# Linear attention on one core: the first chunk begins with the values, and the identity has a load of its own

## What is computed

```python
xn = _layernorm(x)                      # x: 2048 x 512
q = silu(xn @ Wq); k = silu(xn @ Wk); v = silu(xn @ Wv)
# chunks of 128 tokens, 16 heads of 32
scores = einsum('bchd,bshd->bhcs', qb, kb) * D
o_intra = einsum('bhcs,bshd->bchd', scores, vb)
o_inter = einsum('bchd,bhde->bche', qb, S) * q_decay
S_new = chunk_decay * S + einsum('bshd,bshe->bhde', kb * k_decay, vb)
gate = (xn @ Wg1) @ Wg2
out = rmsnorm_per_head((o_intra + o_inter) * sigmoid(gate)) * w @ Wo
```

## Time and profile before

| | us |
|---|---|
| median of 3 runs | 1657.27 |
| the 3 runs | 1653.48 to 1657.48 |
| profiled execution, its own time | 1654.82 |
| profiled execution, its span | 1653.0 |
| busy: PE / DVE / ACT / POOL | 1547.6 / 997.4 / 593.1 / 640.0 |

### The profile page before, as it was taken

How to read it: one execution, slowest core, us unless ns; L and a number is a source line. 1 busy time by engine, 2 the same in 40 slices (tenths; PEclk the granted TensorE clock), 3 DMA queues, 4 the chain that set the end, 5 groups by cost and what they waited for, 6 DMA issues and landing times. The chain is left out here.

```text
span 1653.0 us, 22088 instructions
## 1 busy us (share of the span) xinstructions
PE 1547.6 (94%) x7906; PEld 1077.0 (65%) x7906; DVE 997.4 (60%) x1719; ACT 593.1 (36%) x1124; POOL 640.0 (39%) x534
## 2 busy tenths in 40 slices
PE   5999899999999999997989999959999998999998
PEld 4887445455544555553767888847777776788887
DVE  7774888787778788863445566545564455232322
ACT  3121245555555555554222222253424232222221
POOL 4000277858868886700336766513120201000000
PEclk9999799999999999999899999979999998999999
DMA  6887645444525464301751222153030231420210
GB/s 234 249 256 205 136 124 120 105 116 133 119 62 161 120 141 102 104 16 45 258 193 58 78 70 64 52 180 128 1 128 1 77 81 61 147 100 3 102 52 26
DMA packets 104299, 182.07 MB, mean 110 GB/s; under 512 B 28696, under 2 KB 45080, under 8 KB 103540
## 3 DMA queue, kind: packets, MB, share of 16 engines
q1 hardware_dynamic: 87032, 119.20, 25.2%
q0 software_dynamic: 13520, 53.85, 11.3%
q10 hardware_dynamic: 3640, 7.61, 1.3%
HBM read 118.62 MB, written 61.74 MB: 109 GB/s over the span
## 5 line engine op out<-in xcount | busy, mean ns | idle before, releaser
L1072 ACT ACTIVATE att_probs<-att_ring 128x512 f32<-128x512 f32 (+3 forms) x640 | 298.1, 536 | 286.8 <-DVE att_ring L1103 142.9
L1094 DVE TENSOR_REDUCE att_maxes<-att_ring 128x2 f32<-128x1024 f32 (+7 forms) x366 | 339.3, 948 | 71.2 <-PE att_ring L992 61.3
L1025 PE MATMUL att_outp<-att_probs,att_vs 128*64 128x512 f32 (+3 forms) x1280 | 276.0, 553 | 0.3 <-ACT att_att L1056 0.3
L1025 PEld LDWEIGHTS att_outp<-att_probs,att_vs 128*64 128x64 f32 x1280 | 79.0, 138 | 122.4 <-issue 70.7
L1804 DVE TENSOR_TENSOR glu_hid<-glu_sig,glu_u 128x512 f32<-128x512 f32 x44 | 30.3, 688 | 140.6 <-PE glu_u L1744 140.6
L1013 PE MATMUL att_ring<-route_wah,route_wbh 102*128 102x512 f32 (+2 forms) x320 | 104.6, 402 | 4.7 <-DVE att_maxes L1094 3.7
L992 PE MATMUL att_ring<-route_wbh,route_wah 100*128 100x512 f32 (+2 forms) x320 | 101.0, 399 | 8.2 <-DVE att_maxes L1094 5.6
L1013 PE MATMUL att_ring<-moew_wal,moew_wbl 102*128 102x512 f32 (+2 forms) x320 | 102.2, 401 | 6.0 <-DVE att_maxes L1094 6.0
L2374 POOL TENSOR_TENSOR lin_sig<-lin_o_copy,lin_sig 128x512 f32<-128x512 f32 x16 | 20.4, 1277 | 208.4 <-ACT lin_o_copy L2234 208.4
L992 PE MATMUL att_ring<-moew_wbl,moew_wal 100*128 100x512 f32 (+2 forms) x320 | 96.2, 377 | 3.8 <-DVE att_maxes L1094 1.9
L1013 PEld LDWEIGHTS att_ring<-route_wah,route_wbh 102*128 102x128 f32 x320 | 55.0, 191 | 67.1 <-issue 39.1
(11 more groups left out here) (294 smaller groups left out, 3457.6 us busy)
## 6 DMA issues: line engine op xcount, KB each, us to landing
att_q_raw<-in_w POOLq DMA_DIRECT2D x48, 352.0 KB, 4.3
w_ternary<-att_q_out POOLq DMA_DIRECT2D x24, 352.0 KB, 2.8
tail_up<-w_ternary SPq DMA_DIRECT2D x22, 256.0 KB, 5.0
xn<-qkv_x SPq DMA_DIRECT2D x4, 1024.0 KB, 7.9
q_hi<-qkv_hi SPq DMA_DIRECT2D x16, 256.0 KB, 3.8
q_lo<-qkv_lo SPq DMA_DIRECT2D x16, 256.0 KB, 4.5
k_hi<-qkv_hi SPq DMA_DIRECT2D x16, 256.0 KB, 2.9
k_lo<-qkv_lo SPq DMA_DIRECT2D x16, 256.0 KB, 3.8
```

The source lines that it names most:

```text
L1025: last = pe.matmul(outp[v_cols(h), off:CH], vs[p % 2][:, kt, v_cols(h)], probs[:, g % 4, h, off:CH], start=kt == 0, stop=kt == TT * (c + 1 ...
L1072: act.activation(probs[:, g % 4, h, off:CH], ring[:, rg.banks["score", g][h], off:CH], ACT.Exp).then_inc(exped, 1)
L1094: last = dve.tensor_reduce(maxes[:, hs, t, g:g + 1], banks[:, :, 0:width], AX.X, ALU.max)
```

## The change

The first chunk of the linear attention is made in the order v, q, k instead of q, k, v (the later chunks keep q, k, v). The weight that is split during the experts' stage is now Wv instead of Wq, and the stage itself splits Wq, Wk, Wg1, Wo in that order. The first chunk's normalised tiles are turned into the PSUM tile `lin_wide` (one bank for each tile) by `first_turn`, not through the ring, and the loop over the tiles of v waits for one tile's low part at a time. The identity stands last in the constants and has a transfer and a semaphore of its own, `ident_in`; TensorE's block begins with the wait for it alone, and the wait for `g2_in` moves to `gates`. On ScalarE a root of `lin_eps` into `lin_warm` stands ahead of the wait for the statistics, and the decays (`q_decay`, `k_decay16`, `c_decay`) now come ahead of the first high parts.

```diff
-    HT, WQ_AT = FT // 2, range(2, 2 + 3 * KT, 3)
+    HT, WV_AT = FT // 2, range(2, 2 + 3 * KT, 3)
...
-            for kind, count, late in (("q", KT, 0), ("k", KT, 0), ("v", TT, 0), ("gk", 1, 0),
-                                      ("norm", TT, -1), ("out", TT, 1), ("turn", KT, 0)):
+            inner = [("q", KT, 0), ("k", KT, 0), ("v", TT, 0)]
+            if c == 0:
+                inner = [inner[2], *inner[:2]]
+            for kind, count, late in (*inner, ("gk", 1, 0), ("norm", TT, -1), ("out", TT, 1), ("turn", KT, 0)):
+                if kind == "norm" and c == -1:
+                    continue
...
-        order = ("k", "v", "g1", "o")
+        order = ("q", "k", "g1", "o")
...
-            for dst, src in ((cst, cst_d[:, P:]), (ld_p, decay_p_d), (nw, norm_w_d)):
-                sp.dma_start(dst[:], src).then_inc(s_in, 16)
+            rest = NC - P
+            sp.dma_start(ident, cst_d[:, P + rest:]).then_inc(ident_in, 16)
+            for dst, src in ((cst[:, 0:rest], cst_d[:, P:P + rest]), (ld_p[:], decay_p_d), (nw[:], norm_w_d)):
+                sp.dma_start(dst, src).then_inc(s_in, 16)
...
-                wait_taken(sp, "norm", c, TT - 1)
+                if c:
+                    wait_taken(sp, "norm", c, TT - 1)
+                else:
+                    sp.wait_ge(first_low, TT)
...
+            def first_turn():
+                for t in range(TT):
+                    pe.wait_ge(norm.normed, t + 1)
+                    for k in range(KT):
+                        last = pe.transpose(wide[:, t, k * P:(k + 1) * P], x[:, t, k * P:(k + 1) * P], ident)
+                    last.then_inc(first_turned, 1)
...
-            pe.wait_ge(s_in, 3 * 16)
-            pe.wait_ge(g2_in, 16)
-            pe.wait_ge(zeroed, 2)
-            norm_turn(0)
+            pe.wait_ge(ident_in, 16)
+            first_turn()
             for c in range(NCH):
-                wait_taken(pe, "norm", c, TT - 1)
+                if c:
+                    wait_taken(pe, "norm", c, TT - 1)
+                else:
+                    for t in range(TT):
+                        pe.wait_ge(first_low, t + 1)
+                        projected("v", 0, t, "v", True)
+                    pe.wait_ge(s_in, 3 * 16)
+                    pe.wait_ge(zeroed, 2)
+                    ws.wait(pe, KT)
...
+            def first_high():
+                for t in range(TT):
+                    act.wait_ge(first_turned, t + 1)
+                    act.activation(xh[:, :, t * P:(t + 1) * P], wide[:, t, :].rearrange("p (k n) -> p k n", n=P), ACT.Copy
+                                   ).then_inc(norm.xh_ready, 1)
...
             act.wait_ge(zeroed, 2)
+            act.activation(warm[:], eps[:], ACT.Sqrt)
             norm.take_root(act, 0)
-            norm_high(0)
-            split(("k",))
             act.wait_ge(s_in, 3 * 16)
...
+            first_high()
+            split(("q",))
+            for t in range(TT):
+                take(v[:, t, :], ACT.Silu, "v", 0, t)
+            split(("k",))
...
                 else:
-                    split(("v", "g1"))
+                    split(("g1",))
...
+            def first_low_parts():
+                for t in range(TT):
+                    s = slice(t * P, (t + 1) * P)
+                    dve.wait_ge(norm.xh_ready, t + 1)
+                    dve.tensor_tensor(xl[:, :, s], wide[:, t, :].rearrange("p (k n) -> p k n", n=P),
+                                      xh[:, :, s].bitcast(F32), ALU.subtract).then_inc(first_low, 1)
...
-    parts += [p == c, P - 1 - p]
+    parts += [P - 1 - p, p == c]
```

More of the change, by code:

```diff
@@ L1388, in experts_stage @@
                                      for n, k in (("gathered", 2), ("fetched", 3), ("stored", 3)))
-        wq_raw = st.sb("wq_raw", [P, D])
-        wq_in, wq_high, wq_low, next_in = (st.sem(n) for n in ("wq_in", "wq_high", "wq_low", "next_in"))
+        wv_raw = st.sb("wv_raw", [P, D])
+        wv_in, wv_high, wv_low, next_in = (st.sem(n) for n in ("wv_in", "wv_high", "wv_low", "next_in"))
         x_turned, xh_ready, xl_ready = st.sem("x_turned"), st.sem("xh_ready"), st.sem("xl_ready")
@@ L1514, in _ @@
                     x_high(j + 2)
[L1515 to L1518, removed]
+                if j in WV_AT:
+                    k = WV_AT.index(j)
+                    act.wait_ge(wv_in, (k + 1) * 16)
+                    act.activation(carried.h[:, k, :], wv_raw[:], ACT.Copy).then_inc(wv_high, 1)
         @block.vector
@@ L1590, in _ @@
                     down_bias(j + 1)
[L1591 to L1595, removed]
+                if j - 1 in WV_AT:
+                    k = WV_AT.index(j - 1)
+                    dve.wait_ge(wv_high, k + 1)
+                    dve.tensor_tensor(carried.l[:, k, :], wv_raw[:], carried.h[:, k, :].bitcast(F32),
+                                      ALU.subtract).then_inc(wv_low, 1)
             finish(NT - 1)
@@ L1871, in lightning_stage @@
         cst = st.sb("cst", [P, NC])
[L1872 removed]
+        at = np.cumsum([0, P, P, P, HD, KT * P, 1, P])
         dist, ld_f = carried.dist[:], carried.ld_f
[L1874 removed]
+        causal, cpos, diag, msel, spread, kpos, ident = (cst[:, a:b] for a, b in zip(at[:-1], at[1:]))
         names = ("q", "k", "v", "o")
         wh, wl = {}, {}
[L1877 to L1878 removed]
+        wh["v"], wl["v"] = carried.h, carried.l
+        for i, n in enumerate(("q", "k")):
             wh[n], wl[n] = kept.weights(i)
@@ L1914, in lightning_stage @@
         s_in, zeroed, expd, masked = st.sem("s_in"), st.sem("zeroed"), st.sem("expd"), st.sem("masked")
-        g2_in = st.sem("g2_in")
+        g2_in, ident_in = st.sem("g2_in"), st.sem("ident_in")
+        first_turned, first_low = st.sem("first_turned"), st.sem("first_low")
         scored, score_taken = st.sem("scored"), st.sem("score_taken")
@@ L2039, in gates @@
                 wait_taken(pe, "gk", c)
+                if c == 0:
+                    pe.wait_ge(g2_in, 16)
                 if c:
@@ L2109, in _ @@
                 if c == 0:
-                    ws.wait(pe, KT)
+                    ws.wait(pe, 2 * KT)
                 for m in range(KT):
@@ L2114, in _ @@
                     spread_inverses(c - 1)
[L2115 to L2118, removed]
+                    for t in range(TT):
+                        projected("v", c, t, "v", True)
                 if c == 0:
@@ L2215, in _ @@
                     act.wait_ge(o_made, c * NI)
+                    for t in range(TT):
+                        take(v[:, t, :], ACT.Silu, "v", c, t)
                 else:
                     split(("o",))
-                for t in range(TT):
-                    take(v[:, t, :], ACT.Silu, "v", c, t)
                 if c:
@@ L2310, in _ @@
             norm.normalize(dve, 0)
-            norm_low(0)
+            first_low_parts()
             dve.wait_ge(s_in, 3 * 16)
```

13 lines of the change are left out of this document (6 added, 7 removed).

## The result

The changed kernel took 1642.51 us (median of 4 runs, 1638.83 to 1642.89), the kernel before, run with it, 1657.38 (1653.48 to 1662.84). The ratio is 0.9919, with a 95% interval of 0.9896 to 0.9942. The direction was right; the ratio makes 0.0081 x 1657.38 = 13.4 us, more than the 8.7 us that I had summed.

The account below looks back on a forecast made before the run. TensorE, busy for 94% of the span, was taken as the bound. Terms 5.65 + 1.35 + 1.8 - 0.1 = 8.7 us gave 1646.1 (profiled) or 1648.6 (median); forecast 1647.5 us, range 1644 to 1652.

Parts of the forecast that it names:

- Start of the products: Seam into the linear attention: first product at 1091.9 instead of 1097.55, a gain of 5.65 us.
- The root ahead: ScalarE before the first normalised tile: Sqrt's table loaded ahead brings the root 0.16 us earlier.
- The clock: TensorE's first products: clock rises 0.4 to 2.0 us after the first, losing 0.6 instead of 1.95; gain 1.35 us.
- Rival 1: The clock's run counts only from the first product, not the transposes; total gain 6.95 us, 1649.1; chance 0.18.
- The wait in k: First chunk's k: without four high parts on ScalarE ahead of the take, TensorE's wait goes; gain 1.8 us.
- Later in the chunk: Wo's four high parts now stand between the last k and the take of gk; cost 0.1 us.
- The identity's own load: Head of the stage: identity there by 1085.2 at the latest, three us before needed; no separate gain summed.
- the bound of 4.0: Lower bound, in us, on the gain at the products' start, for ScalarE 1.65 us later than worked out.
- rival 4: Lead given back in the chunk by late Wo or gk; 4 of 8.7 us lost, 1652.8; chance 0.07.
- Rivals 2 to 5: Includes rival 2, rival 3, rival 4; the fifth: ScalarE stands at late Wo before gk, slower, 1661.6, chance 0.03.
- rival 3: Wait in k stays because chunk 1's root waits for late x; gain 6.9 us, 1649.2; chance 0.06.
- rival 2: ScalarE holds the products' start; 1.5 us of delay beyond its cover gives gain 7.2, 1648.9; chance 0.06.

Follow-up runs that it names:

- run 26: Not a label but a count: the unedited kernel before was run 26, 34 and 16 times beside the experiments; medians 1654.11, 1653.32 and 1652.98 us.
- Wg2's wait alone: Kernel before with only TensorE's wait for Wg2 moved from the head of its list to the gates; 1651.32 us, ratio 0.9980.
- the runs with a raised clock: Changed kernel with extra TensorE work ahead of the real transposes: 14 identity transposes (twice) or 24 products; ratios 0.9915, 0.9940 and 0.9940.
- taken last: Changed kernel with the wait for Wg2 put back at the head of TensorE's list; 1647.91 us, ratio 0.9979.
- again: Changed kernel, unedited, run a second time beside the kernel before; 1644.68 us, ratio 0.9950.
- the identity's 14 ahead: Changed kernel with 14 transposes of the identity ahead of the real ones, run twice; 1642.62 us (ratio 0.9915) and 1642.46 us (0.9940).
- the 24 early products: Changed kernel with 24 products of the carried distances with themselves at the head of TensorE's list; 1644.63 us, ratio 0.9940.

## Why the prediction was right in the mechanism and wrong in the number

**The step that failed** is the last one, the range: it "begins at the largest gain ... from the own time 1654.8, or 1644.8, less a little of scatter". I took the three runs from 1653.48 to 1657.48 for the whole scatter and gave it 0.8 us below. The kernel before was run 26, 34 and 16 times beside these experiments, each time on another chip. It lay between 1646.11 and 1667.53, with medians of 1654.11, 1653.32 and 1652.98; the base of my forecast (half-way between 1654.82 and 1657.27) was 2 to 3 us above them. The changed kernel's 19 runs in three comparisons have a median of 1644.33 and began at 1638.83; the four of the first comparison were 1.8 us below that median. Nine of the 19 lie below my range and two above it. With base 1654.1 and the gain below, the expected time is 1645.0, inside the range but only 1 us from its end; the first comparison fell outside by scatter that I had not allowed for. Where that scatter lies is shown: the first memset falls anywhere from 1069.9 to 1082.7 in the span, while the stretch behind it repeats to 1.6 us for one kernel. Ahead of the memset the attention takes from 599.5 to 609.0 us in the 13 profiles. TensorE's idle time in it differs from 15.4 to 21.6 us, its time at half clock from 23.9 to 34.2. If a us at half clock costs half a us (an estimate, from the 0.49 of the prediction), the attention less both is 568.8 to 572.1 in all 13, so the two together cover most of its scatter. What makes them vary stays open; no experiment was made on it.

**The gain.** From the first memset to the end the mean of the three profiles of the changed kernel is 565.1 against 574.2: 9.1 us, where the sum said 8.7. By the first k decay it is 63.6 - 54.1 = 9.5, and the way from there to the end is 509.6 to 511.4 us in all 13 profiles, so the lead is kept. By its steps:

- *Start of the products, 5.65.* Measured 18.7 - 12.6 = 6.1. The tile is normalised when I said (9.3 after the memset against 9.2), and the transposes took 3.1 to 3.3 instead of 3.7. The step is mis-sized by the tails of the two rows of eight: a row of 16 is 3.65 us long at half clock, but the product behind it starts 3.30 after its start. I had taken off 0.2 us. ScalarE's chain came as worked out, 0.7 us ahead of need and not 1.0.
- *The root ahead, 0.16.* Against the two profiles of before, the first normalised tile is begun 0.2 to 0.3 us earlier (8.6 us after the memset, not 8.9), about as worked out. But the part isn't one number: without the root ahead it was 0.8. The hidden wait was 0.35 and 0.37 us in the profiles of before, 0.92 and 1.12 in the two others.
- *The clock, 1.35.* In three profiles the rise came 0.2 us before the first product, 0.4 after, and 1.9 after: a loss of 0, 0.2 and 0.9 us at 0.49 each, where I took 0.6. The kernel before rose 4.2 us after its first product in both profiles and lost 2.0, so the gain is some 1.7 on average, by an estimate from these rows. Rival 1, with 2.0 to 2.8 us in each execution, is out. But the reason that I gave, that an unbroken run raises the clock, isn't all of it: see below.
- *The wait in k, 1.8.* Right: at the first k decay 1.8 us come back with 1.96 us of work on ScalarE.
- *Later in the chunk, -0.1.* Too small to be told, but nothing larger happened: in the changed kernel's waits up to the first k decay neither the take of lin_kt nor Wo's rest stands, and gk's take has 0.2 us.
- *The identity's own load:* nothing, as the argument had it that all constants land before the tile.

With 6.1, 1.7, 1.8 and -0.1 the steps make 9.5, what the first k decay shows. Two side sums of the prediction were wrong without touching the forecast. With 1.0 us of cover, a ScalarE 1.65 us late delays the start by 0.65 only, so the bound of 4.0 should have been 5.0. And rival 4's 1652.8 goes by the median, where the other rivals go by the half-way base; by that it is 1651.4.

Rivals 2 to 5 did not happen in the changed kernel; rival 3's mechanism showed with Wg2's wait alone. ScalarE (rival 2) is close behind, as the runs with a raised clock show. The drain of 1.38 us that the Trainium skill has beside a table switch (ScalarE: Activation LUTs, What ACT_TABLE_LOAD costs) appears as no time here either: table, decays and the first high part follow without a gap in 2.86 us.

The parts aren't independent. Of 9.5 us at the first k decay, Wg2's wait is worth 3.9 when it is taken last (3.5 of it at the start of the products) and 2.6 when taken first. The two executions also differ in the rise of the clock and in the statistics (1.0 us later in the second), so the difference isn't the order's alone; the 1.2 us by which the wait in k grew are part of it.

## What to carry to other kernels

An engine's list that begins with one wait for all transfers is held by the last of them; read the row's releaser and ask when its data is first used. After a pause, begin with the product that needs one tile and not all, and look at what the next engine in line has to do just before it is needed. And before giving a range, find the scatter of the whole program, not of the stage: measure a change in one stage from a mark inside that stage, since single comparisons of one and the same kernel here ran from 0.9919 to 0.9950.

## What the hardware showed that I had not expected

The time from the first work after a pause to the rise of the clock isn't fixed. In the changed kernel the clock rose 2.9, 5.2 and 3.7 us after the first transpose, with the same instructions. These are windows of two of the profiles:

```profile
1088.00:1089.00 1.00, 1.00 (x5) 0.81 (x4) 0.79 (x2) 0.74 (x3) 0.00 (x0) 0.50 0.00 0
1089.00:1090.00 1.00, 1.00 (x5) 0.77 (x4) 1.00 (x2) 1.00 (x3) 0.46 (x1) 0.61 0.00 0
```

```profile
1088.00:1089.00 1.00, 1.00 (x6) 1.00 (x5) 0.84 (x2) 0.74 (x2) 0.00 (x0) 0.51 0.30 102
1089.00:1090.00 1.00, 1.00 (x8) 0.86 (x7) 0.84 (x2) 1.00 (x3) 0.00 (x0) 1.00 0.00 0
```

The upper pair (again) has transposes from 1084.58 and rises at 1089.8, the lower (first profile) from 1086.03 and rises at 1089.0. Nor does a short wait always hold it back: it rose 10 us after the first transpose in both profiles of before, and 4.3 us after it with Wg2's wait alone, with the same wait of 0.56 us between the same transposes. There the rise came ahead of the wait of 1.41 us, and that wait did not lower the clock again. The Trainium skill (TensorE: Matmul & The Clock Gate, The HAM clock gate) calls the count of slow matmuls run-variable; the three profiles of the changed kernel agree, with its first products all fast in one and at half clock for 1.9 us in another. What decides between 4.3 and 10 us stays open. Transposes alone do raise it: with the identity's 14 ahead, the clock rose 2.8 us after the first of them in the second run, before any product, and 5.1 us in the first, amid the real ones. After the 24 early products it stayed up over a pause of 0.92 us.
